# Decoder kernel: the memory stage with new shares for the engines, and totals over partitions made on TensorE

## What is computed

```python
x = x + mixer(_layernorm(x), ...)                            # state-space mixer
# memory read: hidden = _layernorm(x), memory_tokens = ctx
scores  = where(mask, hidden @ ctx.T * scale, -1e30)         # memory stage
x = x + softmax(scores) @ ctx
# routed FFN: of every batch the 128 rows with the largest weight
weights = _layernorm(x) @ W_r + b_r;  topk(weights, 128);  gather, gelu FFN, scatter
x = x + attention over the batch axis
# fp8 product: ctx in blocks of 128 x 128
q = (wb * (448 / amax(abs(wb)))).astype(float8_e4m3);  wq = q * (amax / 448)
x = x + quantised(_layernorm(x)) @ wq.T
x = x + ternary FFN;  weight scale = mean(abs(w)) over a whole weight
```

## Time and profile before

| | us |
|---|---|
| median of 3 runs | 1294.31 |
| lowest and highest | 1290.65, 1297.1 |
| the profiled execution, its own time | 1289.9 |
| span of its core in the trace | 1288.2 |
| mixer | about 0 to 508 |
| memory stage, first score tile to the FFN's first product | about 508 to 758 |
| FFN | about 758 to 853 |
| last stage | about 853 to 1288 |

### The profile page before, as it was taken

How to read it: one execution, slowest core, us unless ns; L and a number is a source line. 1 busy time by engine, 2 the same in 40 slices (tenths; PEclk the granted TensorE clock), 3 DMA queues, 4 the chain that set the end, 5 groups by cost and what they waited for, 6 DMA issues and landing times.

```text
span 1288.2 us, 15225 instructions
## 1 busy us (share of the span) xinstructions
PE 1103.3 (86%) x5168; PEld 779.7 (61%) x5168; DVE 896.8 (70%) x1720; ACT 530.9 (41%) x962; POOL 534.0 (41%) x766
## 2 busy tenths in 40 slices
PE   4899999999999997956868479976889989899785
PEld 3777888888788875423434267755456565465432
DVE  5678777877877774566666658666767777877753
ACT  5433343433333330211212037643267667576533
POOL 5465446545554462132323301013555545645510
PEclk9899999999999998988889679988989999999887
DMA  8100000000000011610000025410000000000000
GB/s 306 39 1 1 1 1 1 1 1 1 1 1 1 1 33 45 247 68 0 33 1 0 1 106 183 153 33 0 1 9 9 17 9 17 9 9 17 9 17 17
DMA packets 16685, 45.09 MB, mean 35 GB/s; under 512 B 2784, under 2 KB 3808, under 8 KB 14304
## 3 DMA queue, kind: packets, MB, share of 16 engines
q1 hardware_dynamic: 16608, 44.12, 9.5%
HBM read 39.92 MB, written 4.19 MB: 34 GB/s over the span
## 4 chain that ended last, share of the span: by engine, by line
PE 50%; DVE 19%; issue 13%; POOL 11%; ACT 7%; DMA 1%; ACTq 0%; DVEq 0%; POOLq 0%
PE bank L367 39%; PE bank L375 3%; PE bank L443 3%; DVE da_hi L820 1%; POOL prod L2044 1%; DVE o L1297 1%; PE bank L434 1%; DVE fm L1370 1%; DVE spare L1065 1%; ACT g L1740 1%; POOL eu L2079 1%; DVE b_u L1002 1%; POOL y L1921 1%; POOL fm L2110 1%; DVE wq L992 1%
## 5 line engine op out<-in xcount | busy, mean ns | idle before, releaser
L367 PE MATMUL bank<-win_hi,a_uT_hi 128*128 128x512 f32 (+1 forms) x320 | 128.4, 401 | 7.7 <-DVE win_lo L774 4.7
L367 PE MATMUL bank<-win_lo,a_uT_hi 128*128 128x512 f32 (+1 forms) x320 | 122.5, 383 | 0.0
L367 PE MATMUL bank<-win_hi,a_uT_lo 128*128 128x512 f32 (+1 forms) x320 | 121.6, 380 | 0.0
L1900 POOL TENSOR_TENSOR da_lo<-upto,dt 128x256 fp32r<-128x256 f32 x128 | 104.2, 843 | 3.4 <-PE bank L367 3.3
L820 DVE TENSOR_TENSOR da_hi<-upto,dth 128x256 fp32r<-128x256 f32 x128 | 79.4, 668 | 0.0
L367 PE MATMUL bank<-f,fqT 128*128 128x512 bf16 (+1 forms) x384 | 78.9, 362 | 0.0
L367 PEld LDWEIGHTS bank<-win_hi,a_uT_hi 128*128 128x128 f32 x320 | 62.3, 195 | 21.9 <-issue 6.3
L367 PE MATMUL bank<-ctx,pT 128*128 128x512 f32 x128 | 72.7, 722 | 0.7 <-ACT pT L1592 0.7
L1500 ACT ACTIVATE ex<-bank 128x48 f32<-128x48 f32 x16 | 3.4, 211 | 164.7 <-PE bank L408 164.7
L367 PEld LDWEIGHTS bank<-win_lo,a_uT_hi 128*128 128x128 f32 x320 | 62.2, 194 | 12.6 <-issue 2.9
L443 PEld LDWEIGHTS bank<-xs,wgt 128*128 128x128 f32 x512 | 62.6, 196 | 10.8 <-issue 6.7
(11 more groups left out here) (303 smaller groups left out, 3075.7 us busy)
## 6 DMA issues: line engine op xcount, KB each, us to landing
wchunk<-w_in SPq DMA_DIRECT2D x32, 256.0 KB, 6.2
stage<-f_in SPq DMA_DIRECT2D x4, 1408.0 KB, 7.4
x<-x_in SPq DMA_DIRECT2D x16, 256.0 KB, 5.9
land<-win_in SPq DMA_DIRECT2D x4, 1024.0 KB, 6.5
wq<-ctxT_in SPq DMA_DIRECT2D x4, 1024.0 KB, 8.7
ctx<-ctx_in SPq DMA_DIRECT2D x4, 1024.0 KB, 5.9
out<-x SPq DMA_DIRECT2D x16, 256.0 KB, 2.0
first_stage<-f_in SPq DMA_DIRECT2D x2, 1408.0 KB, 13.9
```

Source lines behind the costliest of these rows:

```text
L367: made = e.matmul(bank, a, b, start=start and n == 0, stop=stop and n == len(pairs) - 1)
L1900: made = e.tensor_tensor(da_lo[(2 * G + k) % 4][:], upto[:].unsqueeze(1).broadcast_to([P, HG // 2, P]), dt[m % 2][:, 3, h:h + HG // 2].uns ...
```

## The change

Every engine's loop of the memory stage is written anew with 23 passes (`n`), each piece with its own lag (`t3` is tile n - 3). What moves:

- Means: `add_mixed` and `add_recalled` (VectorE) also write the row sum of their result. `mean_u`, `mean_v` on GpSimd turn it into minus the mean; ScalarE squares and sums (`square_u`, `square_v`); GpSimd makes scale and shift in three small steps (`deviation_u`, `deviation_v`); ScalarE writes the normalised tile (`normal_u`, `normal_v`).
- fp8: VectorE keeps mask and magic number (`memory_magic`); add and subtract go to GpSimd (`round_add`, `round_off`).
- Maxima over partitions: a transpose on TensorE, a maximum on VectorE (`memory_tops`), a transpose of the broadcast maxima back. Totals of ternary weights: a product with ones on TensorE.
- Four small steps behind `pick_slots` go from VectorE to GpSimd (`keep_factors`).

```diff
# TensorE
+            def turn_limits(n):
+                b, c = divmod(n, TPB)
+                if c: return
...
+                w.wait_ge("limits_made", b + 1)
+                e.transpose(bank[0:KD * KD, 0:P], bscale[:, b, 0, :], ident[:]).then_inc(sig("limits_turned"), 1)
+            def spread_tops(n):
...
+                w.wait_ge("tops_made", b + 1)
+                e.transpose(banks.of["limits", b][:, P:P + KD * KD], tops[0:KD * KD, b:b + 1].broadcast_to([KD * KD, P]),
+                            ident[0:KD * KD, 0:KD * KD]).then_inc(sig("limits_turned"), 1)
...
+            def ternary_total(n):
+                bank = banks.claim(w, ("total", n), "total_kept", n + 1)
+                w.wait_ge("abs_summed", ABS * (n + 1))
+                e.matmul(bank[:, 0:ABS], ones[:], abs_sum[:], start=True, stop=True).then_inc(sig("totalled"), 1)
# VectorE
-                moments(i, c_st, c_mv[i % 2], "v_moments")
+                                       op0=ALU.mult, op1=ALU.add, accum_out=c_mv[i % 2][:, 0:1]).then_inc(
+                    sig("x_recalled"), 1)
...
-            def memory_fp8(b, n):
+            def memory_magic(b, n):
...
+                w.wait_ge("q_step", 4 * (2 * b + n) + 1)
# ScalarE
+            def square_rows(i, name, mv):
...
+                w.wait_ge(f"{name}_mean", i + 1)
+                e.activation(b_squares[:], x[i][:], ACT.Square, bias=mv[:, 1:2], accum_out=mv[:, 2:3]).then_inc(
+                    sig("squared"), 1)
+            def normal_u(i):
+                w.wait_ge("u_rstd", 3 * i + 3)
...
+                e.activation(b_u[i % 2][:], x[i][:], ACT.Identity, bias=mv[:, 4:5], scale=mv[:, 3:4]).then_inc(
+                    sig("u_ready"), 1)
# GpSimd
-                e.partition_all_reduce(bscale[:, b, 1, :], bscale[:, b, 0, :], P, ABSMAX).then_inc(sig("sum_all"), 1)
-                e.partition_all_reduce(fs[:, 4 * n + 3:4 * n + 4], fs[:, 4 * n:4 * n + 1], P, SUM).then_inc(
+            def row_deviation(i, name, mv, scale, shift, read):
+                w.wait_ge("squared", squared_at[name, i])
...
+                e.tensor_scalar(scale, mv[:, 2:3], 1.0 / D, EPS, ALU.mult, ALU.add).then_inc(sig(f"{name}_rstd"), 1)
+                e.tensor_tensor(scale, scale, mhalf[:, 0:1], ALU.pow).then_inc(sig(f"{name}_rstd"), 1)
+                e.tensor_scalar(shift, mv[:, 1:2], scale, 1.0, ALU.mult, ALU.mult).then_inc(sig(f"{name}_rstd"), 1)
+            def round_add(b, n):
+                w.wait_ge("fp8_magic", 2 * b + n + 1)
+                e.tensor_tensor(half_memory(b, n), half_memory(b, n), qtmp[:], ALU.add).then_inc(sig("q_step"), 1)
+            def round_off(b, n):
+                w.wait_ge("q_step", 4 * (2 * b + n) + 2)
```

More of the change, by code:

```diff
@@ L569, in gather, with turn_pick @@
                 made.then_inc(sig("route_turn"), 1)
-            def turn_pick(b):
+            def turn_pick(n):
+                b, c = divmod(n, TPB)
+                if c < TPB - 1:
+                    return
                 bank = banks.claim(w, ("place", b), "route_kept", 3 * b + 3)
                 turn(bank, pick[:].rearrange("p c s -> p (c s)"), TPB, ident).then_inc(sig("route_turn"), 1)
[L575 to L589, removed]
+            for n in range(NT + 7):
+                t0, t1, t2, t3, t4, t5, t6, t7 = (n - lag if 0 <= n - lag < NT else None for lag in range(8))
+                if t3 is not None:
+                    turn_p(t3)
+                if t2 is not None:
+                    scores(t2)
+                    turn_limits(t2)
+                if t6 is not None:
+                    gather(t6)
+                if t1 is not None:
+                    turn_u(t1)
+                if t3 is not None:
+                    recall(t3)
+                if t2 is not None:
+                    spread_tops(t2)
+                if t7 is not None:
+                    turn_pick(t7)
+                if t4 is not None:
+                    spread_weights(t4)
+                if t5 is not None:
+                    positions(t5)
             accs = [banks.claim(w, ("acc", b), "blk_ready", b + 1) for b in range(BATCH)]
@@ L1093, in pick_slots, with low_gathered @@
                 made.then_inc(sig("picked"), 1)
[L1094 to L1103, removed]
+            def low_gathered(n):
+                b, c = divmod(n, TPB)
+                if c < TPB - 1:
+                    return
                 slots = slice(b * SLOTS, (b + 1) * SLOTS)
@@ L2030, in gpsimd_program @@
-            ternary_total(0)
-            scale_up(BATCH - 1, 1)
-            scale_down(BATCH - 1, 0)
-            scale_down(BATCH - 1, 1)
-            ternary_total(1)
-            ternary_total(2)
+            for n in range(NT + 7):
+                t0, t1, t2, t3, t4, t5, t6, t7 = (n - lag if 0 <= n - lag < NT else None for lag in range(8))
+                if t4 is not None:
+                    mean_v(t4)
+                if t6 is not None:
+                    quantise(scale_up, t6, 1)
+                if t0 is not None:
+                    mean_u(t0)
+                if t1 is not None:
+                    hide_masked(t1)
+                if t4 is not None:
+                    quantise(round_add, t4, 0)
+                    deviation_v(t4)
+                if t3 is not None:
+                    quantise(scale_up, t3, 0)
+                if t4 is not None:
+                    quantise(round_off, t4, 0)
+                if t0 is not None:
+                    deviation_u(t0)
+                if t6 is not None:
+                    quantise(round_add, t6, 1)
+                if t4 is not None:
+                    quantise(scale_down, t4, 0)
+                if t6 is not None:
+                    quantise(round_off, t6, 1)
+                    quantise(scale_down, t6, 1)
+                if t7 is not None:
+                    keep_factors(t7)
@@ L2038, in attend_odd @@
+            for half in range(2):
+                for step in (scale_up, round_add, round_off, scale_down):
+                    step(BATCH - 1, half)
             def attend_odd(n):
```

413 lines of the change are left out of this document (245 added, 168 removed).

## The result

The two kernels, run side by side, gave 1292.48 us before (median of 4, 1286.97 to 1297.1) and **1224.22 us** after (median of 4, 1220.93 to 1226.37); ratio 0.947, interval 0.943 to 0.952. The profiled execution took 1226.37 with a span of 1224.7.

A forecast was written before the change was run, and what follows sets the result against it. No engine was full; VectorE's strict order was late in the memory stage. From 1289.9 us, 49.4 less in the body and 10.7 in the tail (60.1 together), plus 2 in the FFN, gave 1231.8; predicted 1231, range 1209 to 1257.

The forecast's parts named there:

- Start, +1.7: First u tile of the memory stage: its new path through GpSimd and ScalarE was to cost 1.7 us more.
- Body, 99.9 us of TensorE work and 17 of stalls and slow clock: From 557.3 to tile 15's recall: 12 us stall in three batches, 5 for slow recalls (4.93, not 3.60); before, 168.0 us.
- The place: Fourth pass of a batch: `deviation_v` behind `round_add`, then the dot product, delays `spread_weights`; 4 us of stall a batch.
- the small steps at their low values: GpSimd's small steps in the memory stage: power 0.55 and root's first step 0.19, not the means 0.91 and 0.36.
- the dot product's hold: VectorE's dot product in the fourth pass waits for GpSimd's `round_off`, about 2 us of the 4 us stall.
- Tail, 5.4 us to the router's weight: Last recall to the router's last weight: 5.4 us instead of 16.1, without the all-reduce, so 10.7 us less.
- The second part: From the router's last weight to the FFN's first product at 757.93: nothing gets shorter.
- FFN, +2: FFN: VectorE steps held by eight large GpSimd steps instead of four; 2 us more.
- Last stage, 0: Last stage starts with what it needed before: no change, 0 us.
- GpSimd busiest, over 75% of the stage: Sign in the profile after: GpSimd busiest of the three engines beside TensorE, over 75% of the memory stage.
- VectorE loses about 3.3 us a tile: Memory stage: statistics, aggregates, normalised tiles and a copy leave VectorE; with fp8 steps gone, 40.7 us a batch falls to 24.
- VectorE's strict order: Memory stage before: no engine full, VectorE late; TensorE stood 24.8 us for `b_u`, GpSimd 25.0 for statistics.

The follow-up runs named there:

- the order without the maxima: Changed kernel with the all-reduce, the statistics and the magic add and subtract back, normalised tiles still on ScalarE: 1256.42 us, ratio 0.973.

## Why the prediction was right, and where it was not

The time was 1231 predicted, 1224.2 measured (1226.4 in the profiled execution, whose span is 63.5 us shorter; 58.1 were forecast). By its steps:

- **Start, +1.7.** The first u tile came at 511.04 (before at 511.44), and the scores of tile 5 at the same 553.7 as before: nothing.
- **Body, 99.9 us of TensorE work and 17 of stalls and slow clock.** The last recall ends at 668.1 (the next row of TensorE starts at 668.06), 110.8 us behind 557.3: 11 us of stalls and no slow recall, 6 less than counted. The period was 40.0 (I said 38 to 42).
- **The place** was right: the router's weights of the fourth pass. So were 2.4 for a plain add (2.35) and the small steps at their low values (0.25 to 0.31 and 0.55 to 0.59 in the mean). The subtract took 2.54. Of the 4 us of stall in this place the dot product's hold was to be about 2; the stall was 0.8 to 1.1 and the hold 1.0 (1.68 less 0.69).
- **Tail, 5.4 us to the router's weight.** The bias starts at 673.08, 5.0 us behind 668.1. The second part, called unchanged, was 15.6 and not 16.5.
- **FFN, +2.** It was 97.7, against 93.6 before (where the first product with `blk` started at 851.49) and 93.1 with the last add and subtract on VectorE: +4. The mechanism was right: a VectorE step held for GpSimd's. The size was not: the one held row I had gave 2 us, and here `half_lo` (5.20 for two) and `hT_lo` were held in a row. The granted clock of the stage was also 0.98, where it was 1.00 before and in the run with the last batch on VectorE.
- **Last stage, 0.** From the first product with `blk` to the end it took 438.3 us, before 436.7.
- **GpSimd busiest, over 75% of the stage.** Wrong: 102.5 of the 180.7 us from 508 to the FFN, 57%, with VectorE at 104; in the window of one batch the two are level at 29.4 and 29.5 of 40. That VectorE was busy 29.5 a batch and not 24 (the terms named there give 22.6) is due to held steps: the dot product 1.30 in the mean and not 0.69, the first small step of `invert_sum` 0.55 and not 0.16, one of `pick_slots` 1.38 and not 0.17, together 5.2 us a batch.

So the time came out right partly by luck: 6 us of stalls counted too many, 2 of the start and 1 of the tail are set off in part by 2 too few in the FFN and 2 in the last stage.

The step that failed is one that the sum did not need: "VectorE loses about 3.3 us a tile ... from 40.7 us a batch it falls to about 24 and is no bound". I took it for the cause of the shorter period. With all 40.7 us back on VectorE the period is 42 and the time 1224.5. From the kernel before, the maxima by TensorE give 14.8 us (shown); from there to the kernel with everything on VectorE are 52.4 us, in which the order differs, with the four small steps and the ternary totals. In that step VectorE's 16.5 us of waits a batch went to none and the batch from 58.7 to 42.0; three batches make 50 of the 52.4 us. A kernel with those places alone changed was not run. In the new order the shares given away bring 0.3 us in all, less than can be told: about 3.6 in the stage, where VectorE was full, against 4.5 lost in the FFN. What they would bring in the old order was not run either. There VectorE's work and waits filled the batch, so less work may have shortened it too; what is shown is that the shares are not needed for the gain. The order could also be read ahead: the prediction named "VectorE's strict order" as late, but priced the body by the new stalls and never asked which part of the change took the old ones away.

What stays open is the last 3 us a batch between 40.0 and TensorE's 37. Four kernels that took away one stall (maxima, weights) all got one of the same or a greater size at the next step of the ring of waits from TensorE over the other engines back to it.

## What to carry to other kernels

Where an engine works in a strict order and is busy 70% of a batch while others wait for it, add up its own waits. If work and waits fill the batch, look first at the instructions it stands before with others queued behind, and move those later or their inputs earlier. Here that was enough, and the work taken off the engine brought 2 us a batch once the waits were gone. A reduction over partitions of a few values belongs on TensorE if GpSimd's queue is on the path, and its cost is to be read as the idle time around it, not as its row. When work goes to GpSimd, list the VectorE steps that will run beside its long ones: here a bias of 0.23 us on the chain took 2.18.

## What the runs showed of the hardware

- An all-reduce of 128x16 on GpSimd: 0.39 us busy, with at least 5.6 us of idle time ahead and at least 6.7 behind in each of its twelve rows in three kernels (the one before, the all-reduce back, the order without the maxima). The longest are 10.1 and 9.8, in which real waits may be counted.
- VectorE's dot product of 128x512 takes 0.69 us in each row of the kernel before. Its means over the stage were 1.30 (changed), 1.03 (add and subtract back) and 0.70 (statistics back too); the longest rows beside a GpSimd step are of 2.74. The mask step with one input went from 0.66 to 2.25 beside a scaling.
